# Second feed-forward part computed by lists of 64 places per expert

## The reference, cut to what matters

```python
# x: 2048 x 128, E = 64 experts, I = 64 hidden, TOP_K = 8, CAPACITY = 64
gu = x @ shared_gate_up_w
shared = _silu(gu[:, :Is]) * gu[:, Is:] @ shared_down_w          # Is = 256
shared = shared * jax.nn.sigmoid(x @ shared_gate_w)
w, idx = jax.lax.top_k(jax.nn.softmax(x @ gate_w), TOP_K)
w = w / jnp.sum(w, axis=-1, keepdims=True)
pos = ...            # how many earlier (token, choice) pairs chose the same expert
slot = jnp.minimum(pos, CAPACITY)
buf = jnp.zeros((E, CAPACITY + 1, H)).at[e_flat, slot].set(x[tok])
gu_e = jnp.einsum('ech,ehf->ecf', buf, expert_gate_up_w)
act = _silu(gu_e[..., :I]) * gu_e[..., I:]
out_e = jnp.einsum('eci,eih->ech', act, expert_down_w)
y = out_e[e_flat, slot] * w_flat[:, None]
y = jnp.where((pos < CAPACITY)[:, None], y, 0).reshape(T, TOP_K, H).sum(axis=1)
return y + shared
```

## Time and profile before

| | us |
|---|---|
| median of 3 runs (3393.77 to 3406.36) | 3402.42 |
| the profiled execution, own time | 3400.11 |
| its span in the trace | 3398.3 |
| PE busy | 2907.7 (86%) |
| DVE busy | 2289.8 (67%) |
| ACT busy | 1498.6 (44%) |
| POOL busy | 1214.8 (36%) |
| mean granted clock of TensorE, as a share of full | 0.911 |

### The profile page before, as it was taken

How to read it: one execution, slowest core, us unless ns; L and a number is a source line. 1 busy time by engine, 2 the same in 40 slices (tenths; PEclk the granted TensorE clock), 3 DMA queues, 4 the chain that set the end, 5 groups by cost and what they waited for, 6 DMA issues and landing times. The chain is left out here.

```text
span 3398.3 us, 42635 instructions
## 1 busy us (share of the span) xinstructions
PE 2907.7 (86%) x16486; PEld 1768.6 (52%) x16486; DVE 2289.8 (67%) x3415; ACT 1498.6 (44%) x2848; POOL 1214.8 (36%) x1096
## 2 busy tenths in 40 slices
PE   6989998799799985699978888768888989998499
PEld 3544555577544442477755656555553333334367
DVE  4444436699777612699967777369956757765688
ACT  1333333366356600366635555247753334333155
POOL 2322311266311000266654445047713434442054
PEclk8889988799889977799989999789998989998799
DMA  2000000133200010255522212223300000001032
GB/s 84 1 1 1 1 32 34 63 124 122 74 1 1 1 79 13 59 123 124 123 63 64 62 54 76 87 108 140 136 13 1 1 0 1 1 1 42 0 126 87
DMA packets 32717, 180.66 MB, mean 53 GB/s; under 512 B 7297, under 2 KB 7553, under 8 KB 16673
## 3 DMA queue, kind: packets, MB, share of 16 engines
q1 hardware_dynamic: 32514, 177.93, 16.9%
HBM read 161.33 MB, written 15.47 MB: 52 GB/s over the span
## 5 line engine op out<-in xcount | busy, mean ns | idle before, releaser
L302 PE MATMUL ps<-parts 128*128 128x512 f32 (+7 forms) x7520 | 1558.6, 412 | 168.3 <-DVE parts L316 73.6
L302 PEld LDWEIGHTS ps<-parts 128*128 128x128 f32 (+3 forms) x7520 | 1022.8, 190 | 746.9 <-issue 230.9
L316 POOL TENSOR_TENSOR work<-work 128x512 f32<-128x512 f32 x480 | 630.4, 1314 | 987.3 <-DMA work<-scr_w 482.7
L312 ACT ACTIVATE work<-ps 128x512 f32<-128x512 f32 (+4 forms) x898 | 523.2, 608 | 579.3 <-PE ps L302 559.9
L316 DVE TENSOR_TENSOR parts<-work,parts 128x512 fp32r<-128x512 f32 x468 | 651.3, 1403 | 34.5 <-ACT parts L312 33.8
L332 DVE TENSOR_REDUCE fw_sb<-ps 128x2 f32<-128x1024 f32 (+3 forms) x384 | 415.2, 1087 | 274.7 <-PE ps L302 273.7
L302 PE MATMUL ps<-work 128*32 128x256 f32 (+5 forms) x2396 | 364.1, 421 | 36.1 <-DMA work<-work 27.6
L312 ACT ACTIVATE parts<-work 128x512 fp32r<-128x512 f32 x468 | 294.7, 631 | 186.0 <-DVE work L316 171.9
L312 ACT ACTIVATE fw_sb<-ps 128x512 f32<-128x512 f32 (+5 forms) x394 | 204.6, 536 | 309.7 <-PE ps L302 268.7
L302 PEld LDWEIGHTS ps<-work 128*32 128x32 f32 (+2 forms) x2396 | 138.4, 137 | 197.9 <-issue 135.2
L306 PE MATMUL ps<-wc_sb,fw_sb 128*128 128x128 f32 x1128 | 209.3, 299 | 36.9 <-DVE work L341 11.7
(11 more groups left out here) (127 smaller groups left out, 2880.9 us busy)
## 6 DMA issues: line engine op xcount, KB each, us to landing
work<-scr_w SPq DMA_DIRECT2D x74, 1024.0 KB, 4.6
work<-scr_w SPq DMA_DIRECT2D x72, 512.0 KB, 6.3
work<-scr_sk SPq DMA_DIRECT2D x64, 128.0 KB, 2.7
scr_sp<-wr_sb SPq DMA_DIRECT2D x64, 128.0 KB, 2.2
fw_sb<-in_f SPq DMA_DIRECT2D x1, 6528.0 KB, 18.3
fw_sb<-in_f SPq DMA_DIRECT2D x1, 5376.0 KB, 15.3
fw_sb<-in_f SPq DMA_DIRECT2D x1, 4608.0 KB, 18.2
scr_sk<-work SPq DMA_DIRECT2D x64, 64.0 KB, 1.7
```

Of the source, the lines that this page charges most:

```text
L302: return self.e.matmul(o, l, r, start=start, stop=stop) if self.e else Unwritten()
L312: return self.e.activation(o, i, f, bias=bias, scale=scale)
L316: return self.e.tensor_tensor(o, a, b, op) if self.e else Unwritten()
```

## The change

The experts' products are no longer made for all tokens. `Experts` keeps the two shared units alone (`first=32` shifts to their weights). `Routing1` now writes two things: `rows`, a table with one row of 192 numbers per token (128 features, normed, and 64 weights), and `places`, for each expert the place (1 to 64) of each token or 0, as bf16. The transposes of tokens and the shared factor come ahead of the choice, the norm of the weights (two reductions' worth of DVE work) comes behind the places, and the weights are not cut by the capacity. `Store1` writes both to DRAM, in five transfers in place of two: the table in pieces of 512 and 256 bytes.

The new stage `Sparse` takes the 32 pairs one per step, five steps deep. In step n: SP loads the pair's two rows of places, each spread over 64 partitions (`B`, 2 x 256 KB). DVE compares them with the number of the partition (`match`) and multiplies by `code`, the token's number from 1: `C` is then 128 places x 2048 tokens with the token's number where they meet, and `accum_out` sums it, so that `at` holds the number of the token in each place. POOL fetches the 128 rows of the table by an indirect DMA (`gather`). PE transposes the 128 x 128 features, ACT and DVE split them, POOL splits the weights, PE makes gate and up for 128 columns, ACT takes Silu of the two diagonal blocks alone, DVE multiplies, PE makes the down product turned round (places on the partitions), ACT and DVE scale it by the weight and split it into `Y`. `add_pe` multiplies `Y` by `C` for all four chunks and adds to banks 0 to 3 over all pairs: eight matmuls of 512 columns. At the end DVE multiplies the banks by 1 / number (`inverse`) and adds to `xT`.

```diff
+class Sparse(Stage):
+    N = 32
+    def __init__(self, k, tab, pos, stored):
...
+        self.C, self.H = ring(5, T), ring(3, P)
+        self.X, self.F, self.Y = ring(3, 256), ring(3, 256), ring(3, 256)
+        self.inverse = A.get(T)
+        self.B = [self.inverse[:, 1024 * i:1024 * i + 1024].bitcast(BF16) for i in range(2)]
...
+    def pe(self, e):
+        for n in self.steps():
+            if self.due(n - 2):
+                self.turn_pe(e, n - 2)
+            if self.due(n - 4):
+                self.add_pe(e, n - 4, 0)
+            if self.due(n - 3):
+                self.down_pe(e, n - 3)
+            if self.due(n - 2):
+                self.up_pe(e, n - 2)
+            if self.due(n - 4):
+                self.add_pe(e, n - 4, 1)
...
+    def add_pe(self, e, p, i):
+        e.wait_ge(*k.made_v[t, "output parts", p])
+        for c in range(NC):
+            ins = e.matmul(k.ps[c][:, :], R(self.Y[p % 3][:, tile(i)]), R(self.C[p % 5][:, ch(c)]),
+                           start=p == 0 and i == 0, stop=p == self.N - 1 and i == 1)
...
+    def match_dve(self, e, p, h):
+        e.wait_ge(*self.spread[p % 2][p])
+        e.wait_ge(*self.coded["in"])
+        e.wait_ge(*k.summed[t, "added", p - 5, 1])
+        c = slice(1024 * h, 1024 * h + 1024)
+        e.match(R(self.C[p % 5][:, c]), self.B[p % 2][:, c], k.cst("place"), self.code[:, c], self.acc[p % 4][:, h:h + 1]
...
+    def match(self, o, a, s, b, accum):
+        return self.e.scalar_tensor_tensor(out=o, in0=a, scalar=s, in1=b, op0=ALU.is_equal, op1=ALU.mult, accum_out=accum)
+    def gather(self, o, table, at):
+        return self.e.indirect_dma_start(o, None, table, bass.IndirectOffsetOnAxis(at, 0))
...
+    def dve(self, e):
...
+            if self.due(n - 2):
+                e.wait_ge(*k.made_a[t, "token parts", p])
+                e.tt(R(x[:, 128:256]), self.bank(0), x[:, 0:128], ALU.subtract).then_inc(*k.made_v.up((t, "token parts", p)))
+            if self.due(n - 3):
+                e.wait_ge(*k.made_a[t, "hidden parts", p])
+                e.tt(R(f[:, 128:256]), self.Z[p % 3], f[:, 0:128], ALU.subtract).then_inc(*k.made_v.up((t, "hidden parts", p)))
+            if self.due(n):
+                self.match_dve(e, n, 0)
+            if self.due(n - 3):
+                e.wait_ge(*k.made_a[t, "output parts", p])
+                e.stt(R(y[:, 128:256]), self.bank(3), self.w[p % 4], y[:, 0:128], ALU.mult, ALU.subtract
+            if self.due(n):
+                self.match_dve(e, n, 1)
+                e.wait_ge(*k.made_v[t, "matched", n, 1])
+                e.wait_ge(*self.fetched[n % 4][n - 4])
+                e.tt(self.at[n % 4], a[:, 0:1], a[:, 1:2], ALU.add).then_inc(*k.made_v.up((t, "token", n)))
+            if self.due(n - 2):
+                e.wait_ge(*k.summed[t, "up", p])
+                e.wait_ge(*k.made_a[t, "gate", p, 1])
+                e.tt(self.Z[p % 3], self.S[p % 3], self.bank(2), ALU.mult).then_inc(*k.made_v.up((t, "hidden", p)))
...
+        for c in range(NC):
+            x, y = k.xT[:, ch(c)], self.tmp[:, ch(c % 2)]
+            e.tt(y, k.ps[c][:, :], self.inverse[:, ch(c)], ALU.mult)
+            e.tt(x, x, y, ALU.add)
...
+    def act(self, e):
...
+            if self.due(n - 3):
+                e.wait_ge(*k.made_v[t, "hidden", p])
+                e.activation(R(self.F[p % 3][:, 0:128]), self.Z[p % 3], ACT.Copy).then_inc(*k.made_a.up((t, "hidden parts", p)))
+            if self.due(n - 2):
+                e.wait_ge(*k.summed[t, "turned", p])
+                e.activation(R(self.X[p % 3][:, 0:128]), self.bank(0), ACT.Copy).then_inc(*k.made_a.up((t, "token parts", p)))
+            if self.due(n - 1):
+                e.activation(R(self.H[p % 3][:, 0:384]), k.fw[:, p * 384:p * 384 + 384], ACT.Copy
+            if self.due(n - 3):
+                e.wait_ge(*k.summed[t, "down", p])
+                e.activation(R(self.Y[p % 3][:, 0:128]), self.bank(3), ACT.Copy, scale=self.w[p % 4]
+            if self.due(n - 2):
+                e.wait_ge(*k.summed[t, "gate", p])
+                for h in range(2):
+                    r = slice(64 * h, 64 * h + 64)
+                    e.activation(self.S[p % 3][r, r], self.bank(1)[r, r], ACT.Silu).then_inc(*k.made_a.up((t, "gate", p, h)))
...
+    def pool(self, e):
+        for n in self.steps():
+            if self.due(n - 1):
+                e.tt(R(h[:, 384:768]), k.fw[:, p * 384:p * 384 + 384], h[:, 0:384], ALU.subtract)
+            if self.due(n - 2):
+                e.wait_ge(*self.fetched[p % 4][p])
+                e.tt(self.ww[p % 4], g[:, 128 + 2 * p:130 + 2 * p], k.cst("either"), ALU.mult)
+                e.tt(w, self.ww[p % 4][:, 0:1], self.ww[p % 4][:, 1:2], ALU.add)
+            if self.due(n):
+                e.wait_ge(*k.made_v[t, "token", n])
+                e.gather(self.G[n % 4], self.tab, self.at[n % 4]).then_inc(*self.fetched[n % 4].up(n))
...
+    def sp(self, e):
+        e.dma_start(self.code, bass.AP(code.tensor, 0, [[0, 128], [1, T]])).then_inc(*self.coded.up("in"))
+        e.wait_ge(*self.stored["places"])
+        for p in range(self.N):
+            if p > 1:
+                e.wait_ge(*k.made_v[t, "matched", p - 2, 1])
+            for h in range(2):
+                e.dma_start(self.B[p % 2][64 * h:64 * h + 64, :], bass.AP(self.pos.tensor, (2 * p + h) * T, [[0, 64], [1, T]])
+        e.wait_ge(*k.made_v[t, "matched", self.N - 1, 1])
+        e.dma_start(self.inverse, bass.AP(code.tensor, T, [[0, 128], [1, T]])).then_inc(*self.coded.up("inverse"))
...
 class Routing1(Routing):
-        self.norm_dve(e)
         for h in range(2):
+            c = ch(h)
             e.wait_ge(*k.summed[t, "places", h])
-            self.step(e, e.ts(self.sel[:, h * 512:h * 512 + 512], self.Mb[h][:, :], 64.5, ALU.is_lt))
-        self.step(e, e.tt(self.w, self.w, self.sel, ALU.mult), (t, "weights"))
+            self.step(e, e.stt(self.lg[:, c], self.Mb[h][:, :], 64.5, self.sel[:, c], ALU.is_lt, ALU.mult))
+            self.step(e, e.tt(self.er[:, c], self.lg[:, c], self.Mb[h][:, :], ALU.mult), (t, "taken", h))
+        self.step(e, e.tt(self.w, self.w, self.sel, ALU.mult))
+        self.step(e, e.reduce(st[:, 16:32], self.v3(self.w), ALU.add))
+        self.step(e, e.reciprocal(st[:, 16:32], st[:, 16:32]))
+        self.step(e, e.tt(view(self.rows[:, 128:], [192, 16], [1, E]), self.v3(self.w), self.b3(st[:, 16:32]), ALU.mult),
+                  (t, "weights"))
...
+class Store1(Stage):
+    def act(self, e):
+        e.wait_ge(*self.stored["places"])
+        e.wait_ge(*self.stored["weights"])
+    def sp(self, e):
+        e.dma_start(self.tab[0:1, :], r.none).then_inc(*self.stored.up("none"))
+        e.dma_start(rows(0, 128), view(r.rows, [192, 16], [1, 128])).then_inc(*self.stored.up("table"))
+        e.dma_start(self.scr[64:65, :], r.sg).then_inc(*self.stored.up("shared"))
+        e.dma_start(self.pos[:, :], r.places).then_inc(*self.stored.up("places"))
+        e.dma_start(rows(128, 64), view(r.rows[:, 128:], [192, 16], [1, 64])).then_inc(*self.stored.up("weights"))
...
 def ffn_stages(k, l):
-        units = [([2 * p, 2 * p + 1], 0) for p in range(32)] + [([64], 0)] * 2
-        X = Experts(k, 1, A, k.lnT, units, scr, stored, ACT.Silu, True)
+        X = Experts(k, 1, A, k.lnT, [([64], 0)] * 2, scr, stored, ACT.Silu, True, first=32)
+        return before + [Parts(k, X), r, Store1(k, r, scr, pos, tab, stored), X, Sparse(k, tab, pos, stored)]
```

More of the change, by code:

```diff
@@ L2830, in middle_pe @@
             ins.then_inc(*k.summed.up((t, "places", h)))
+        for c in range(NC):
+            e.wait_ge(*k.made_a[t, "tokens", c])
+            e.wait_ge(*k.made_v[t, "taken", c // 2])
+            for i in range(4):
+                ins = e.transpose(k.ps[c][0:64, tile(i)], self.er[:, (4 * c + i) * E:(4 * c + i) * E + E], k.cst("id"))
+            ins.then_inc(*k.summed.up((t, "rows", c)))
     def choose_dve(self, e):
@@ new lines, in choose_dve, with dve @@
+            self.step(e, e.tt(self.er[:, c], self.lg[:, c], self.Mb[h][:, :], ALU.mult), (t, "taken", h))
[4 more added lines that the diff above has]
+                  (t, "weights"))
+    def dve(self, e):
+        k, t, E = self.k, self.tag, self.E
+        self.steps = 0
+        for n in range(2):
+            e.wait_ge(*k.summed[t, "logits", n])
+            self.step(e, e.copy(self.lg[:, ch(n)], self.Mb[n][:, :]), (t, "logits", n))
+        self.choose_dve(e)
@@ L2850, in pe @@
+    def act(self, e):
         k, t = self.k, self.tag
         for c in range(NC):
[L2852 to L2856, removed]
+            e.wait_ge(*k.summed[t, "tokens", c])
+            e.activation(view(self.rows[:, 768 * c:], [192, 4], [1, 128]), view(k.ps[c][:, :], [128, 4], [1, 128]), ACT.Copy
+                         ).then_inc(*k.made_a.up((t, "tokens", c)))
@@ L2857, in act @@
         self.exp_act(e)
-        k, t = self.k, self.tag
         for c in range(NC):
             e.wait_ge(*k.summed[t, "shared", c])
```

(11 more changed lines are left out.)

188 lines of the change are left out of this document (168 added, 20 removed).

## The result

| | before | after |
|---|---|---|
| median of 4 runs, us | 3404.39 (3393.77 to 3406.88) | 3307.27 (3304.48 to 3309.63) |
| ratio, 95% interval | | 0.9715 (0.9697 to 0.9744) |
| the profiled execution, own time | 3400.11 | 3309.63 |
| its span | 3398.3 | 3307.8 |

The forecast was 3319, with 3280 to 3372 as its range; the likeliest case came true in size and sign. By its steps it was less good: two errors of opposite sign nearly cancelled inside one of its terms, and that is what the experiments are about.

A forecast was written before the change was run, and what follows sets the result against it. DVE was taken as the bound, lengthened by waiting beside POOL. The part's 300.8 us became 28.0 shared, 0.5 border, 185.4 new stage and 4 routing and store, 217.9; saving 82.9 gave 3317, as a median 3319, range 3280 to 3372.

The forecast's parts named there:

- the likeliest case: Whole kernel: DVE's work plus port contention set the new stage's step at 5.1 us, 3319 us in all; chance 0.52.
- store: Store of table and places after the routing: 1.8 MB in small pieces, 13 us taken, between 7 and 22.
- What bounds it, and the lock: Steps of the new stage: DVE's 4.25 us plus 0.85 waiting beside POOL for the shared port, 5.1 us.
- the step that failed: Gather loop in the new stage: needs a step of only 4.55 us, so hidden under the 5.1 us step.
- DVE's own step: DVE's operations for one pair of experts: 4.20 us, 4.25 with its wait for itself; bounds 3.8 and 4.6.
- contention: DVE's second match waits 0.7 us for POOL's subtraction, plus 0.15 for tiny products: 0.85 a step, bounds 0 and 1.4.
- The letter of the lock: Exclusive port lock in each step: all 1.01 us of POOL's subtraction could fall on DVE, giving 5.4 us.
- G: Gather time in the new stage, from start through issue, landing, transpose, ACT copy and semaphores: 4.4 us, upper bound 8.0.
- gather loop binds: Rival in the new stage: G of 8 gives a step of 6.3 us, kernel 3363 us; chance 0.14.
- Places loop: Load of the places for a later match: 4.9 us against 6.1, hidden; as binding rival step 5.8, 3341 us, chance 0.06.
- The clock: Rival in the new stage: TensorE's clock falls to 1.2 GHz, step 5.7 us, kernel 3338 us; chance 0.06.
- What was to show it: Expected trace signs: match near 1.3 us, DVE over 80% busy, PE about 60%, gather landing under 3 us.

The follow-up runs named there:

- order_half: Output parts moved behind match 1 on DVE, against the changed kernel with fetch one step earlier and ACT's token parts before hidden parts: 3299.95 us.

## Why the prediction was right, and where it was not

| term, us | predicted | measured |
|---|---|---|
| routing up to the store | -4.5 | -4.4 |
| store | 13 | 9.2 |
| shared units (border 0.5 included) | 28.5 | 25.2 |
| until the first match | 8.8 | 7.2 |
| first match to the first token parts | 7.5 | 8.5 |
| 30 steps | 153.0 | 146.2 |
| tail with the last DVE operations | 16.1 | 17.1 |
| saved by the changed stretch | 82.9 | 96.3 |

The difference is 3.8 + 3.3 + 1.6 - 1.0 + 6.8 - 1.0 = 13.5, less 0.1 for the routing. Of its 13.4, 5.8 were taken back by scatter elsewhere, which no forecast could hold; 3317 for the profiled execution became 3309.6. Most of the 3.3 in the shared units is the wait for `W`: POOL's first product starts 4.9 us after its issue (1420.07 against 1415.20), and I had carried over 7.4.

**What bounds it, and the lock.** Right for 4.05 of the step's 4.73, which are DVE's work and the port that it shares with POOL; taking POOL's subtraction away gave match 1 its 0.48 back. The other 0.68 is the step that failed, below.

**The mis-sized term: DVE's own step.** I had 4.25 and it is 3.57. The 0.68 too much (the same figure as the idle time, by chance) are in the rows. The read of the accumulator lasts 0.08, not 0.141, and the next instruction starts with it (1486.75 twice), so that a match goes by in 1.20 from start to start and not 1.43: 0.46 for two. And of four short operations (token parts, hidden parts, output parts, token) the next one starts 0.08 before their length is over; against my figures that is 0.30. Against that, the wait for itself before token is 0.11 and not 0.05, and hidden 0.29. I took durations of group means where distances between starts were due, a distinction I had made for matmuls.

**The mis-sized term: contention.** 0.85 forecast, 0.48 measured. The scheme was right (subtraction between the matches, output parts passing beside it). Of the subtraction's 1.01 us 0.27 pass beside output parts, and it still ends 0.68 after match 1 has begun (1487.70 against 1487.02); match 1 is longer by 0.48 only. Where the other 0.2 goes no row shows. The 0.15 for the tiny products is nothing: the step of 4.73 stays without them; the first stands still within match 1, and the second falls beside token and hidden. The letter of the lock, 5.4 a step, was not reached. The Trainium skill, SBUF — State Buffer, section "Who interferes with whom", calls it an exclusive lock; the 1.18 us of a product of 128x2 show that this holds against POOL too, and order_half's 0.27 for 0.27 shows it against DVE.

**The step that failed: the loops "hidden" at 4.55** (4.53 by its own terms). This is the error that the others covered. G was forecast 4.4 and is 5.6: from the token's end 0.61 to POOL's start (0.1 in my sum; without the tiny products 0.27), 0.96 issue (1.2), 3.32 until the transpose starts (2.3), and 0.72 for the transpose and two copies of ACT until DVE's start (0.57 and part of 0.25). Of the 5.6 at most 0.08 is idle (the transpose ends at 1489.48 and ACT's copy of the tokens starts at 1489.56), so the gather loop needs 4.69 a step or little more, and the rival "gather loop binds" was less wrong than its 0.14 says, though it was not the loop that set the pace. What did I did not list at all: ACT's order, which puts a copy that waits for DVE's last operation before one that DVE's first operation waits for. I had added up ACT's work (1.9 us) and seen it lie below DVE's, and not asked in which order it came. It costs 0.68 a step, 21 us in all, of which 11 could be had with two edits that show no gain each. Had DVE's own step been sized rightly and the loop missed, the forecast for a step would have been 3.57 + 0.85 = 4.4. Against the mean of 4.87 the 5.1 was nearer, and that was luck; against the steady 4.73 neither was better by much.

**Places loop.** Hidden, as forecast: no wait of DVE for `scr_places` after the first step, with 3.9 us to landing against 4.3 taken.

**The clock.** It was half a rival. At the start it is 0.50 until 1466 to 1471 us; then it is 1.00 with three short falls, two of them behind a late fetch (1511 to 1521 and 1541 to 1551 us). The third, to 0.78 in 1581 to 1586, has none: there the fetches took 3.8 and 4.4 us. Windows of 5 us around the first:

```profile
1516.00:1521.00 5.00, 5.00 (x17) 4.22 (x17) 3.67 (x10) 1.80 (x6) 4.25 (x5) 0.50 0.30 74
1511.00:1516.00 5.00, 2.58 (x12) 1.67 (x10) 3.17 (x7) 1.00 (x3) 3.54 (x5) 0.89 0.56 146
```

PE had waited 2.42 us for a fetch that took 5.4 us instead of 4.2, and in the next window the clock is 0.50 and PE busy for all of it. The first long step, 5.85 us, is the fetch's. The second, 5.12, is PE's at the low clock:

```profile
1514.27 5.15 PE L306 MATMUL ps<-parts 128*128 128x512 f32 x17
1519.22 0.41 PE L310 MATMUL ps<-wc_sb,work 128*128 128x128 f32 x1
```

The transpose at 1519.22 follows the seventeen matmuls with no wait for a fetch; at a clock of 1.00 the same seventeen took 3.39 us from 1489.23. The kernel with the earlier fetch shows the same without any late fetch: its granted clock falls again and again (mean 0.81 from 1470 to 1580 us, 0.93 here), and its slow steps are 5.0 to 5.1 us. So the clock costs a few tenths of a microsecond in some steps. The prediction had priced it for every step.

**Store.** The lower end was the near one. Its window (share 0.79 of the DMA engines, 205 GB/s) points to the transfer and not to SP's issues; with 1 MB of it moved ahead it took 5.6 us:

```profile
1406.00:1415.00 9.00, 0.00 (x0) 0.00 (x0) 0.00 (x0) 0.00 (x0) 0.00 (x0) 0.50 0.79 205
```

The price per packet that I had from the earlier trace rows was too high for this use. The Trainium skill, DMA: Bandwidth & Descriptors, section "Why small descriptors are slow (HBM only)", gave an estimate of 9, and the measured 9.2 agrees. The estimate took all pieces at 256 bytes, though more than half of the bytes went in pieces of 512, so the agreement is a loose one.

**What was to show it.** Match 1.28 and 1.76 (near 1.3 and a longer one: right); DVE over 80% busy: 80.0% in 1450 to 1590, at the edge; PE about 60%: 73%; landing under 3 us: wrong, 4.2 with the issue in it, 3.3 behind it; first match near 9: 7.2; route's end to shared units 13: 9.2. "It is wrong if DVE idles at the start of each step" did happen, for ACT and not for the transpose.

## What to carry to other kernels

In a software pipeline, an engine's sum of work is only one bound: for each engine draw the loop through every other engine's fixed order, and ask of each instruction what stands before it in its queue that waits for something later. Where two loops are equally long, undoing one shows nothing; test them in pairs before calling either harmless. Size a step by distances between starts, and leave the operation that reads PSUM between two that compete for the shared port: here it cost nothing there.

## What the runs showed of the hardware that was not expected

- An indirect DMA of 128 rows of 768 bytes occupies POOL for 0.96 us, starts 0.27 us behind the token that it waits for (0.61 where POOL's own tiny product ended in between), and lands 4.2 us after its issue starts, 3.3 behind the issue's end; now and then 5.4. The issue takes 0.96 beside DVE's token parts, hidden parts and the start of match 0 and 0.96 behind the last match alike, so the lock does not touch it. The Trainium skill, DMA: Bandwidth & Descriptors, section "Anatomy of one DMA — SWDGE (gpsimd) path", has 2.0 us plus bytes over 436e3, which is an estimate of 2.2 us; the measured 3.3 is half as much again.
- A product of 256 elements on POOL takes 0.19 us alone and 1.18 beside a match of DVE: the lock lengthens an instruction by its neighbour's time, not in proportion to its own.
- A comparison, product and sum over 1024 columns with one bf16 source takes 1.28 us and the read of its sum 0.08, in which the next instruction has already started.
